# The exp of the diagonal key tiles restricted to its live columns in a causal attention and quantised FFN kernel on eight cores

## The reference

```python
def attn(x, WQ, WK, WV, WO):
    Q = split_heads(x @ WQ.T, 16); K = split_heads(x @ WK.T, 16); V = split_heads(x @ WV.T, 16)
    scores = einsum('bhqd,bhkd->bhqk', Q, K) / sqrt(64)
    scores = where(tril(ones((S, S))), scores, -1e9)
    e = exp(scores - max(scores)); attn = e / sum(e)
    out = einsum('bhqk,bhkd->bhqd', attn, V)
    return merge_heads(out) @ WO.T
def ffn(x, w_int8, weight_scale, bias):
    return einsum('bsd,od->bso', activation_quant(simple_rms_norm(x)), w_int8 * weight_scale) + bias
x = layernorm(x + attn(x, WQ, WK, WV, WO))
x = layernorm(x + ffn(x, w_int8, weight_scale, bias))
```

## Time and profile before

| | us |
|---|---|
| runs of the kernel before | 1875.2 and 1912.47, median 1893.84 |
| the profiled execution | 1875.01 |
| its span on the slowest core (core 4) | 1873.4 |
| spans of the other cores | 1867.8 to 1872.9 |
| granted TensorE clock, mean of a core | 0.763 to 0.767 of full speed |

### The profile page before, as it was taken

One profiled execution on the slowest core, in us unless ns is written; L12 is line 12 of the kernel. 1 busy time (PEld: TensorE's weight loads), 2 busy tenths in 40 slices (PEclk: granted clock), 3 DMA queues, 4 the chain that ended last, 5 costly groups with the idle time before them and its releaser, 6 DMA issues.

```text
span 1873.4 us, 24370 instructions; the slowest of 8 cores (1867.8 to 1873.4 us)
## 1 busy us (share of the span) xinstructions
PE 1247.3 (67%) x8646; PEld 596.7 (32%) x8710; DVE 511.6 (27%) x1373; ACT 958.1 (51%) x1172; POOL 300.2 (16%) x567
## 2 busy tenths in 40 slices
PE   0998777777777755656209986777777777556552
PEld 0444333333343322222104432333333333222221
DVE  1001232211111255656200012322111112656462
ACT  0332327788888624343303323277888885243433
POOL 1000222222212101111100002222222111011111
PEclk9999776577777777787659987765777877777775
DMA  9233003000000011111091330030000000111111
GB/s 163 39 46 45 1 1 46 1 1 1 1 1 2 1 45 68 68 68 68 35 160 30 45 45 1 1 46 1 2 1 1 1 1 2 45 68 68 68 45 45
DMA packets 21398, 64.47 MB, mean 34 GB/s; under 512 B 803, under 2 KB 803, under 8 KB 21284
## 3 DMA queue, kind: packets, MB, share of 16 engines
q0 software_dynamic: 16928, 46.14, 12.6%
q1 hardware_dynamic: 4356, 16.78, 2.5%
HBM read 75.50 MB, written 16.78 MB: 49 GB/s over the span
## 4 chain that ended last, share of the span: by engine, by line
PE 40%; ACT 31%; issue 10%; DVE 7%; DMA 5%; POOL 3%; ACTq 2%; DVEq 2%; POOLq 0%
ACT PT L472 24%; PE psall L268 12%; PE psall L313 8%; PE psall L792 8%; DMA wslotA<-wqt 5%; PE psall L374 4%; PE psall L392 4%; POOL PT L486 3%; ACT x L724 2%; ACT x1b L729 2%; ACTq L866 2%; ACT qT L773 2%; PE psall L759 2%; PE psall L418 2%; ACT outst L867 1%
## 5 line engine op out<-in xcount | busy, mean ns | idle before, releaser
L472 ACT ACTIVATE PT<-psall,ebias 128x1024 bf16<-128x1024 f32 x640 | 661.2, 1122 | 284.1 <-PE psall L374 284.1
L392 PE MATMUL psall<-Vx,PT 128*128 128x65 bf16 x4352 | 302.9, 216 | 117.1 <-ACT PT L472 78.2
L374 PE MATMUL psall<-QT,KT 64*128 64x512 bf16 (+3 forms) x1280 | 284.8, 456 | 136.0 <-ACT PT L472 131.5
L486 POOL TENSOR_TENSOR PT<-PT,mask 128x128 bf16<-128x128 bf16 x512 | 207.7, 427 | 750.4 <-ACT PT L472 750.2
L392 PEld LDWEIGHTS psall<-Vx,PT 128*128 128x128 bf16 x4352 | 210.1, 110 | 279.5 <-issue 268.6
L523 DVE RECIPROCAL rinv<-psall 128x4 f32<-128x4 f32 x64 | 11.7, 182 | 683.6 <-PE psall L392 683.6
L268 PE MATMUL psall<-xT,wslotA 128*128 128x512 bf16 x502 | 114.9, 390 | 94.3 <-DMA wslotA<-wqt 93.8
L792 PE MATMUL psall<-wslotB,qT 128*128 128x512 bf16 x496 | 144.5, 459 | 39.7 <-ACT qT L773 39.1
L326 DVE CAST Vx<-psall 128x512 bf16<-128x512 f32 x64 | 44.2, 691 | 392.5 <-PE psall L313 391.5
L604 PE MATMUL psall<-wslotA,OT 128*128 128x512 bf16 x502 | 125.1, 410 | 38.0 <-DVEq L824 34.7
L313 PE MATMUL psall<-wslotA,xT 128*128 128x512 bf16 x494 | 147.6, 470 | 3.9 <-issue 3.8
(11 more groups left out here) (110 smaller groups left out, 812.4 us busy)
## 6 DMA issues: line engine op xcount, KB each, us to landing
xstg<-x SPq DMA_DIRECT2D x16, 1024.0 KB, 6.0
y<-outst POOLq DMA_DIRECT2D x16, 1024.0 KB, 4.3
xT<-xt POOLq DMA_DIRECT2D x8, 1024.0 KB, 22.2
wslotA<-wqt POOLq DMA_DIRECT2D x2, 2048.0 KB, 42.7
wslotB<-wkt POOLq DMA_DIRECT2D x2, 2048.0 KB, 53.8
wslotA<-wvt POOLq DMA_DIRECT2D x2, 2048.0 KB, 17.6
wslotB<-w8t POOLq DMA_DIRECT2D x2, 2048.0 KB, 17.6
wslotA<-wot POOLq DMA_DIRECT2D x2, 2048.0 KB, 18.0
```

Source lines behind the costliest of these rows:

```text
L374: last = eng.matmul(out, lhsT, rhs, start=True, stop=True, skip_group_check=True)
L392: last = eng.matmul(out, lhsT, rhs, start=(i_glob < 2), stop=(i_glob >= n_total - 2), skip_group_check=True)
L472: eng.activation(PT[:, pt * 1024:(pt + 1) * 1024], psall[:, p * 1024:(p + 1) * 1024], AF.Exp, bias=ebias[:, :], scale=0.125).then_inc(sem_ ...
L486: last = eng.tensor_tensor(blk, blk, mask01[:, :], ALU.mult)
```

## The change

The exp of a diagonal tile no longer covers all 1024 columns. For `colo` above 0 the instruction reads and writes, in each of the two heads' 512 columns, only those from `colo` on: 2 x 384, 2 x 256 and 2 x 128 columns for j = 1, 2 and 3. The first diagonal tile (j = 0) and all tiles below the diagonal keep their 1024 columns. No instruction is added, removed or moved on any engine, and no wait changes; three of the `4*qc + 4` exps of each head pair get a smaller shape of two pieces. The columns that are no longer written are those that `emit_pv` and the mask don't read.

```diff
@@ -468,11 +468,23 @@
                         W("s", "t", stv)
-                        def f2(eng, p=p, pt=pt):
-                            eng.activation(PT[:, pt * 1024:(pt + 1) * 1024],
-                                           psall[:, p * 1024:(p + 1) * 1024],
-                                           AF.Exp, bias=ebias[:, :],
-                                           scale=0.125).then_inc(sem_s, 1)
+                        colo = max(0, k - 4 * qc) * 128
+                        def f2(eng, p=p, pt=pt, colo=colo):
+                            if colo == 0:
+                                eng.activation(
+                                    PT[:, pt * 1024:(pt + 1) * 1024],
+                                    psall[:, p * 1024:(p + 1) * 1024],
+                                    AF.Exp, bias=ebias[:, :],
+                                    scale=0.125).then_inc(sem_s, 1)
+                            else:
+                                w_ = 512 - colo
+                                src = ap(psall, p * 1024 + colo,
+                                         (4096, 128), (512, 2), (1, w_))
+                                dst = ap(PT, pt * 1024 + colo,
+                                         (4096, 128), (512, 2), (1, w_))
+                                eng.activation(
+                                    dst, src, AF.Exp, bias=ebias[:, :],
+                                    scale=0.125).then_inc(sem_s, 1)
                         emit("s", f2)
                         expv[u] = bump("s")
```

## The result

The kernel after runs at 1817.9 us in its profiled execution, 3.1% below before: the ratio of after to before is 0.969, with a 95% interval of 0.9679 to 0.9701. The forecast was 1844 us with a range of 1826 to 1865, so the direction was right, and the gain of 57 us is nearly twice the 31 that I had summed, outside the range. Some executions of either kernel are some per cent longer, at a lower clock on the cores of one die, and every comparison here is between executions that are not.

What follows compares the result with a forecast made beforehand. ACT was taken to pace the diagonal tiles, with POOL's masks bounding them after the change. 48 x 0.59 = 28.3 us in qc 1 to 3 plus 3 in qc 0 make 31 off 1875.0: 1844 us, range 1826 to 1865.

Steps and rivals of the forecast that it cites:

- The place and the bound: End of a head pair: POOL's masks take over from ACT as bound, keeping the gain below ACT's 1.26 us.
- The case in which all of ACT's saving lands: Rival, all head pairs: 64 x 1.26 us gained, 1794 us; would need masks of 0.5 us; chance 0.04.
- a head pair that shrinks by over 0.8 us: Sign in the profile after that would prove the forecast wrong on POOL as the bound.
- What stands between two masks: Gaps between POOL's masks, not shown by the trace: gain per head pair from nothing to 0.74 us.
- I take 0.59: Diagonal tiles: four masks without a break take 3.24 us against 3.83, gaining 0.59 us for each head pair.
- the bound from the pair: Masks: eight instructions at 0.38 us start to start need 3.09 us, a gain of 0.74 us per head pair.
- The Trainium skill's rule of a software dispatch for each instruction: Between masks: some 156 ns of dispatch, if bare, would shrink the gain to 0.11 us; not taken.
- qc 0: the step that failed: V groups behind 16 head pairs pay gains back through the clock: 3 us taken, bounds 0 and 9.4.
- My slower rival: V groups and steps at 1.2 GHz throughout: 42 and 19 us lost less 28 gained, 1908 us; chance 0.04.
- my nine to either side: Clock effect on steps below the diagonal in qc 1 to 3: 0 taken, 9 us to both sides.
- The phases outside the attention stay: Rest of the program: no gain, since nothing is added to any queue and no wait is new.

Runs made afterwards that it cites:

- e7: Masks multiplied by DVE in place of POOL, on the kernel before with full exps: 1835.4 us.
- e11: Masks multiplied by DVE in place of POOL, on the changed kernel with narrow exps, timed in more rounds: ratio to before 0.921.
- e1: Only the exp of the fourth diagonal tile narrowed, second and third keep 1024 columns, against the kernel before: 1859.3 us.
- e2: Changed kernel plus one more POOL instruction on scratch data ahead of the fourth mask, in qc 0 alone: 1834.0 us.
- e3: Changed kernel plus two more POOL instructions on scratch data ahead of the fourth mask, in qc 0 alone: 1835.2 us.
- e4: Kernel before plus one more POOL instruction ahead of the fourth mask, in qc 0 alone: 1875.8 us against 1874.0 of a run of before.
- e10: The change in chunks 1 to 3 alone (144 exps), qc 0 keeping full exps, against the kernel before: 1834.6 us.
- e8: Changed kernel with both heads' blocks masked by one POOL instruction of 2 x 128 columns: 1787.6 us, ratio to before 0.954.

## Why the prediction was right and wrong, point by point

**The place and the bound: right.** I had put the gain at the hand-over from exps to masks to PE at the end of a head pair, with POOL taking over as the bound and the rest of ACT's saving turning into idle time. The unbroken row of masks after, and the square of e7 and e11, show it. The case in which all of ACT's saving lands was wrong for this kernel and right for the one with DVE's masks. One sign that I had named was badly chosen: a head pair that shrinks by over 0.8 us was to disprove the bound, and head pairs of qc 3 shrank by 0.8 and those of qc 0 by 1 to 2 while POOL did bound the end.

**What stands between two masks: undersized.** The step was "I take 0.59". The eight instructions take 3.13 us, at the 0.38 us start to start of the pair, through the three waits between the masks. The direct gain is 3.83 - 3.13 = 0.70 us, and the bound from the pair, 3.09 us, was almost exact. A wait that is already met cost POOL next to nothing, 0.04 us over three, as the exps and DVE had shown it for their engines. Over 48 head pairs that is 5 us. The Trainium skill's rule of a software dispatch for each instruction (GPSIMD Engine Reference, section 2.1, Instruction dispatch) did not show as a gap between instructions: two that follow each other start 0.38 us apart with 0.43 of duration each, with a wait between them or without.

**qc 0: the step that failed.** It read: "If PE starts on them earlier against the rise of the clock, more of them runs slow and each gained us is paid back partly or fully ... I take 3, nearer to the first." The mechanism exists: e1, e2, e3 and e4 show that V groups pay back one for one. But I let it run on without an end. It held for mask spans from 4.18 to 3.49 us and was broken at 3.35; the change lands at 3.13. There single V groups run wholly at 2.4 GHz (5.24 us), the interval falls by 1.0 to 2.0 us from its settled value, and the term was 17 us where I had bounded it by 9.4. That bound was the error of method: it assumed that a clock effect can at best take nothing away. The stage had been in step with the clock's alternation, at an interval that was not its own work's, in which 7.7 us of V group stood for 5.2 us of work at the full clock, and that reserve of up to 2.5 us for each head pair was in the earlier trace rows to be seen, on the gain side as much as on the loss side. My slower rival had counted only its loss. Counted from both sides, an estimate of the term's upper bound is 16 x (0.7 + 2.5) = 51 us.

**qc 1 to 3, beyond the masks.** 46 intervals gave 34.9 us, 0.76 each, against 0.70 of direct gain: 3 us are left for the clock, against my nine to either side. qc 1 shows almost none of it (10.85 to 10.17, at 0.61 and 0.56 of the clock); in qc 3 the interval fell by 0.8 us and the clock rose from 0.74 to 0.79.

**The rest: 5 us that I put at nothing.** "The phases outside the attention stay" was wrong. Of the 5.0 us, some 1.4 are not outside the attention at all: the first head pair of each sequence lies before the first stretch and gains its 0.7 us too (in the second sequence, from the last matmul of L268 to the first reciprocal, 22.56 us became 21.87). The larger part, 2.4 and 1.7 us, lies in `ph45` of the two sequences, with the same instructions: the first, up to the second sequence's first matmul, took 329.7 us at a clock of 0.71 and takes 327.3 at 0.73, and the last phase goes from 295.9 at 0.74 to 294.2 at 0.76. This gain goes in the main with the change in qc 1 to 3 (e10), but single cores of before (294.1 us at 0.75) and of e8 (three of eight at 296 and 0.74) have the other value, so it is not the change's alone; what sets it I did not test, and it stays open.

So of the 26 us that were missing, 14 are qc 0, 6.6 the chunks 1 to 3 (5 of them the masks' pace), and 5 the rest.

## What to carry to other kernels

When an engine's instructions are shortened, ask which engine has the least slack behind it: here a saving of 1.26 us met a partner with 0.19 us of pause, and the partner's work, at its own start-to-start time, was the bound to compute. Waits that are already met cost next to nothing on three engines here, so price a chain that becomes the bound by the closest spacing that its rows show, not by its pauses. And where a repeated stage sits at a constant interval while a matmul group in it takes longer than at full clock, neither a saving nor an addition there is worth what it says: it may be absorbed whole, and past some point be multiplied; the bound must reach to the full-clock time of the group, on both sides.

## What was not expected of the hardware

- A stage can hold its interval against changes in its work. From 0.36 us added to 0.33 us removed for each head pair (before, e1, e2, e3, e4), the head pairs of qc 0 settled at one every 13.64 us, in step with a granted clock that alternated between 1.2 and 2.4 GHz, and the same 24 matmuls took 7.37 to 8.06 us.
- The same program is not equally fast on all cores, in good part for this reason: after the change the head pairs of qc 0 in the first sequence came every 11.6 us on five cores and every 12.6 on three, and those three cores are the ones with the longest spans (1811.8 to 1816.3 us against 1804.1 to 1808.8).
- DVE does the two 128-column masks in 0.36 us (e7) where POOL takes 0.81, and PE's waits for masks before L392, 81.4 us in all after the change, came down to 0.9 us in e11.
